# One channel's last group of rows transposed by DMA, the taps folded by ScalarE, and GpSimd's work for a pair in portions of 128 columns

## The reference

```
x      (64, 128, 2048) fp32         batch, channel, time
W      = weights[condition]          one of 16 matrices of 128 x 128 for each batch
x      = x + einsum('bct,bcd->bdt', x, W)
# a diagonal state space layer, for each channel h, with 64 complex modes n:
dtA    = (-exp(log_A_real) + 1j * A_imag) * exp(log_dt)
Ct     = (C[...,0] + 1j*C[...,1]) * (exp(dtA) - 1) / A
K[h,l] = 2 * Re sum_n Ct[h,n] * exp(dtA[h,n] * l)        l = 0..2047
y      = causal convolution of x with K over time, + x * D[h]
y      = y where the time is below the batch's length, else 0
out    = x + y
```

## Time and profile before

| | |
|---|---|
| median of 3 runs | 1088.93 us (1088.23 to 1088.96) |
| the profiled execution | 1082.12 us, its span 1080.3 us |
| granted TensorE clock | 0.996 |
| TensorE busy | 1004.6 us, 93% of the span |
| VectorE busy | 772.3 us, 71% |
| ScalarE busy | 548.5 us, 51% |
| GpSimd busy | 502.7 us, 47% |
| moved by DMA | 304.96 MB, mean 282 GB/s |

### The profile page before, as it was taken

One profiled execution on the slowest core, in us unless ns is written; L12 is line 12 of the kernel. 1 busy time (PEld: TensorE's weight loads), 2 busy tenths in 40 slices (PEclk: granted clock), 3 DMA queues, 4 the chain that ended last, 5 costly groups with the idle time before them and its releaser, 6 DMA issues.

```text
span 1080.3 us, 29253 instructions
## 1 busy us (share of the span) xinstructions
PE 1004.6 (93%) x11632; PEld 739.8 (68%) x11632; DVE 772.3 (71%) x1711; ACT 548.5 (51%) x1166; POOL 502.7 (47%) x545
## 2 busy tenths in 40 slices
PE   8977788777899999999999999999999999999998
PEld 5322234233347888888888788888888888888886
DVE  4989940000017888888888888888888888888885
ACT  2634334244444556556456555555555555555553
POOL 2200042101205556656666665665665665665530
PEclk9999999999999999999999999999999999999999
DMA  8999999999989999999999999999999999999994
GB/s 343 423 423 423 424 422 422 377 424 424 423 326 294 284 271 262 228 227 224 217 239 233 214 238 224 225 234 228 222 232 226 234 221 229 225 225 232 208 223 118
DMA packets 169543, 304.96 MB, mean 282 GB/s; under 512 B 78194, under 2 KB 111346, under 8 KB 161218
## 3 DMA queue, kind: packets, MB, share of 16 engines
q1 hardware_dynamic: 169090, 302.64, 98.4%
q10 hardware_dynamic: 160, 0.26, 0.1%
q0 software_dynamic: 160, 0.20, 0.1%
HBM read 152.37 MB, written 134.41 MB: 265 GB/s over the span
## 4 chain that ended last, share of the span: by engine, by line
PE 74%; DMA 18%; ACT 3%; DVE 2%; issue 2%; SPq 1%; ACTq 0%
DMA u_scratch<-stage 17%; PE bank L590 16%; PE bank L599 15%; PE bank L555 13%; PE bank L541 10%; PE bank L529 7%; PE bank L567 7%; PE bank L596 5%; ACT stage L708 2%; DVE x_t L1001 1%; PE bank L608 1%; DMA x_f<-in_x 1%; DVE st_sb L991 0%; ACT ring L708 0%; DVE u_t L986 0%
## 5 line engine op out<-in xcount | busy, mean ns | idle before, releaser
L590 PE MATMUL bank<-toep,u_t 128*128 128x192 f16 (+1 forms) x3072 | 342.7, 220 | 2.0 <-issue 1.8
L599 PE MATMUL bank<-g_sb,st_sb 128*128 128x256 f16 x1536 | 305.9, 273 | 0.5 <-issue 0.4
L529 PE MATMUL bank<-x_f,w_buf 128*128 128x512 f32 x512 | 237.3, 608 | 57.2 <-ACT stage L708 35.5
L541 PE MATMUL bank<-ident,u_row 128*128 128x128 f32 x1024 | 277.4, 274 | 0.2
L730 ACT ACTIVATE st_sb<-bank 128x128 f16<-128x128 f32 x448 | 123.8, 276 | 289.6 <-PE bank L567 198.0
L590 PEld LDWEIGHTS bank<-toep,u_t 128*128 128x128 f16 x3072 | 231.3, 98 | 16.3 <-issue 2.4
L529 PEld LDWEIGHTS bank<-x_f,w_buf 128*128 128x128 f32 x512 | 93.4, 192 | 192.4 <-issue 109.8
L1016 DVE COPY_PREDICATED o_sb<-mask,u_row 128x512 f32<-128x512 uint8 x256 | 205.8, 804 | 16.6 <-issue 16.5
L986 DVE SCALAR_TENSOR_TENSOR u_t<-bank,u_t 128x512 f16<-128x512 f32 x256 | 176.2, 689 | 37.4 <-ACT u_t L722 35.4
L596 PE MATMUL bank<-toep,x_t 128*128 128x64 f16 x2048 | 188.3, 193 | 1.9 <-issue 1.9
L431 POOL TENSOR_TENSOR lam_sb<-eyes,lam_v 128x512 f16<-128x512 f16 x64 | 75.2, 1176 | 235.7 <-PE bank L567 235.7
(11 more groups left out here) (135 smaller groups left out, 912.6 us busy)
## 6 DMA issues: line engine op xcount, KB each, us to landing
x_f<-in_x SPq DMA_DIRECT2D x64, 1024.0 KB, 19.6
u_row<-u_scratch SPq DMA_DIRECT2D x128, 512.0 KB, 5.7
out<-o_sb SPq DMA_DIRECT2D x254, 256.0 KB, 3.8
u_scratch<-stage SPq DMA_DIRECT2D x50, 1024.0 KB, 17.8
toep<-k_scratch SPq DMA_DIRECT2D x64, 256.0 KB, 6.0
u_scratch<-ring SPq DMA_DIRECT2D x13, 512.0 KB, 14.7
u_scratch<-kept SPq DMA_DIRECT2D x10, 448.0 KB, 7.0
gt_sb<-g_sb SPq DMA_TRANSPOSE x124, 5.4
```

Source lines behind the costliest of these rows:

```text
L529: last = pe.matmul(bank[:, 4 * (n % 2) + k, :], w_buf[n % XS][:, :], x_f[n % XS][:, k * 512:(k + 1) * 512], start=True, stop=True)
L541: last = pe.transpose(bank[:, 4 + q, g * P:(g + 1) * P], u_row[c % 4][:, h, g, tb * P:(tb + 1) * P], ident[:, :])
L590: pe.matmul(bank[:, y, col + tb * P + NM:col + Q], u[:, h, tb, a, rows_], t[:, h, b, NM:Q - tb * P], start=first, stop=False, skip_group_c ...
L599: last = pe.matmul(bank[:, y, col:col + Q], st[:, h, a, gr * ROWS:(gr + 1) * ROWS], g[:, h, b, :], start=False, stop=(m == 2), skip_group_ ...
```

## The change

Four things are done.

1. For the pairs from `TURNED` = 3 on, channel h = 0 (`TH` = 1) no longer has its last group (g = 3) transposed by TensorE: `groups(c, h)` gives 3 instead of 4, and k = 3 and k = 7 return at once. Instead ScalarE (`parts_hi`) and VectorE (`parts_lo`) make the two fp16 parts of these 128 rows x 256 columns from `u_row` into a buffer `parts` of 128 x 512, and SP issues a DMA transpose of it into `u_t` (`transpose_parts`), in slot c for pair c + 1. `inputs_to_state` and the first `first_half` wait for it (`s_pt`). The evacuations of q = 0 and q = 1 take 384 columns instead of 512.
2. `fold_toeplitz` goes from VectorE to ScalarE.
3. GpSimd's operations of a pair are issued in portions of 128 columns: 8 products and 4 subtractions in `outer`, 4 in `outer_lo`, 4 in `make_lambda`, instead of 4, 1, 1 and 1.
4. The orders of ScalarE and VectorE change: ScalarE has "p" and "t" ahead of the pair's first state; VectorE has the two "x" and "p" ahead of it, and "u" (c + 1, 0) and "o" (c - 1, 0) behind the first and second state.

```diff
+TURNED = 3
+TH = 1
+        parts = sb("parts", [P, TH, 2, 2, P], F16)
+        def groups(c, h):
+            return NG - 1 if c >= TURNED and h < TH else NG
...
+            def transpose_parts(c):
+                sp.wait_ge(s_pl, c - TURNED + 1)
+                wait(sp, s_out, 4 * (c - 3))
+                sp.dma_start(ap(u_t[c % 4], (NG - 1) * ROWS, [[NG * ROWS, TH * 4], [1, ROWS]]),
+                             parts[:, :, :, :, :].rearrange("p h b a t -> p (h b a t)"), transpose=True)\
+                    .then_inc(s_pt, 16)
...
+                if TURNED <= c + 1 < PAIRS:
+                    transpose_parts(c + 1)
                 if has(i, c - 1):
                     store_out(i, c - 1, 0)
...
+            PORTIONS = [(h, z) for h in range(2) for z in range(2)]
             def outer(i, c):
-                    for h in range(2):
+                    for h, z in PORTIONS:
                         o = (2 * n + h) * 16
-                        pool.tensor_tensor(out=ap(dst[r], h * Q, [[16, 16], [1, 16]]),
-                                           in0=ap(ta, o, [[1, 16], [0, 16]]),
-                                           in1=ap(tb, o, [[0, 16], [1, 16]]), op=MUL).then_inc(s_gx, 1)
+                        pool.tensor_tensor(out=ap(dst[r], h * Q + z * P, [[16, 8], [1, 16]]),
+                                           in0=ap(ta, o + 8 * z, [[1, 8], [0, 16]]),
+                                           in1=ap(tb, o, [[0, 8], [1, 16]]), op=MUL).then_inc(s_gx, 1)
...
             def transpose_u(i, c, k):
+                if g >= groups(c, q // 2):
+                    return
...
             def inputs_to_state(i, c):
                 pe.wait_ge(s_ul, 4 * n + 4)
+                wait(pe, s_pt, 16 * (n - TURNED + 1))
...
+            def parts_hi(c):
+                for h in range(TH):
+                    act.wait_ge(s_row[c % 4][h], 16 * (c // 4 + 1))
+                wait(act, s_pt, 16 * (c - TURNED))
+                act.activation(parts[:, :, :, 0, :],
+                               u_row[c % 4][:, 0:TH, NG - 1, :].rearrange("p h (b t) -> p h b t", t=P),
+                               ACT.Copy, scale=US).then_inc(s_ph, 1)
...
-                         ("o", c - 1, 0), ("s", c, 1), ("s", c, 2), ("u", c + 1, 1), ("s", c, 3),
+                         ("o", c - 1, 0), ("p", c + 1, 0), ("t", c, 0), ("s", c, 1), ("s", c, 2), ("u", c + 1, 1), ("s", c, 3),
...
+            def parts_lo(c):
+                dve.wait_ge(s_ph, c - TURNED + 1)
+                dve.scalar_tensor_tensor(out=parts[:, :, :, 1, :],
+                                         in0=u_row[c % 4][:, 0:TH, NG - 1, :].rearrange("p h (b t) -> p h b t", t=P),
+                                         scalar=US, in1=parts[:, :, :, 0, :], op0=MUL, op1=SUB).then_inc(s_pl, 1)
...
             def first_half(i, c, part):
                     dve.wait_ge(s_ul, 4 * n + 4)
+                    wait(dve, s_pt, 16 * (n - TURNED + 1))
...
-                steps = (("s", c - 1, 7), ("u", c, 3), ("o", c - 2, 3), ("t", c, 0), ("u", c + 1, 0),
-                         ("o", c - 1, 0), ("s", c, 1), ("x", c, 0), ("s", c, 2), ("x", c, 1), ("s", c, 3),
+                steps = (("s", c - 1, 7), ("u", c, 3), ("o", c - 2, 3), ("x", c, 0), ("x", c, 1), ("p", c + 1, 0),
+                         ("s", c, 1), ("u", c + 1, 0), ("s", c, 2), ("o", c - 1, 0), ("s", c, 3),
```

## The result

The changed kernel takes 1100.1 us (median of 16 runs, 1090.2 to 1108.8) where the kernel before takes 1088.1 (16 runs beside them, 1083.1 to 1092.7): a ratio of 1.0099, interval 1.0075 to 1.0124. One of the changed kernel's runs, the 1108.8, was a slow one and is not in the ratio. Ratios here are formed from the single runs, so they can differ by 0.1 to 0.2% from the quotient of two medians. The forecast was 1083.2, faster. The profiled execution has 1093.7 us of span where before had 1080.3, 13.4 us more.

The account below looks back on a forecast made before the run. TensorE's order of matmuls was taken as the bound; -13.3 (transposes) + 5.1 (late landings) + 2.5 (one early slot) = -5.7 us, so 1088.9 became 1083.2 us, range 1071 to 1103.

Parts of the forecast that it names:

- The transposes: TensorE, pairs 3 to 63: two line 541 transposes fewer in each of 61 pairs, 0.109 us each, -13.3 us.
- ScalarE's pieces: ScalarE's high part and tap fold, ahead of the pair's first state: 0.4 us each, covered by its 1.40 us wait.
- the shorter evacuation: ScalarE: two of four evacuations lose 128 of 512 columns, some 0.1 us each.
- VectorE's low part: VectorE gains the low part, at most 0.69 us, and loses the 1.03 us fold, ending with less work.
- GpSimd at 10 us a pair: GpSimd's 20 portioned instructions take 10 us a pair, between 6.2 and 11.8, fit under 11.4 and cost nothing.
- the fold: VectorE's tap fold, 1.03 us just after a GpSimd subtraction ends, read as waiting for that whole instruction.
- Does the DMA have room for it?: Doubtful step on the DMA engines: about 1.0 us free in a pair; the new transfer takes 0.6, so fits.
- The pair of 12.05 us: Early pair, line 555 at 324.36 and 336.41, taken to carry 0.58 MB more for only 0.4 us.
- The late landings: New DMA transpose landing late: one pair in six by 0.5 us, +5.1 us, and one early slot, +2.5 us.
- the one named for the DMA engines: Rival: DMA engines become the bound through a second hold, 0.55 us a pair, about 1112 us; chance 0.14.
- its sign of recognition: Profile sign of the DMA rival: waits for that DMA in most pairs, landings of 7 us and more on all queues.
- A hold of the engines at each place of a DMA transpose: DMA engines: a second transpose place in each pair, if it makes its own hold, costs 0.3 to 2.4 us.

Follow-up runs that it names:

- e1: The changed kernel with GpSimd's seven whole instructions to a pair again instead of portions: 1146.1 us, ratio 1.059 to the kernel before.
- e3: The kernel before with an added DMA transpose of 128 x 512 fp16 that nobody reads, behind the load of the taps: 1093.7 us, ratio 1.0099.
- e4: The kernel before with the same 128 KB moved by an unread plain DMA copy in the same place: 1088.7 us, ratio 1.0066.
- e7: The changed kernel with output stores cut to the first of four groups, three quarters of the output unwritten: 1064.5 us.
- e8: The kernel before with output stores cut to the first of four groups, three quarters of the output unwritten: 1075.3 us.
- e12: The changed kernel with its DMA transpose from pair 9 on, still behind the taps, and channel 1's store ahead of the table's transposes: 1087.2 us, ratio 1.0065 to before.
- e13: The changed kernel with all transposes on TensorE and channel 1's store ahead of the table's DMA transposes from slot 8 on: 1073.1 us, ratio 0.992 to before.
- e5: The changed kernel with the DMA transpose of the parts from pair 9 on instead of pair 3: 1088.0 us, ratio 1.0034 to the kernel before.
- e10: The kernel before with an unread DMA transpose of 128 x 512 fp16 directly ahead of the table's two: 1095.5 us, ratio 1.0056.
- e14: The changed kernel with channel 1's store, then the parts' DMA transpose, directly ahead of the table's, from pair 9 on: 1063.3 us, ratio 0.984 to before.

## Why the prediction was wrong

**Right.** The transposes: -13.3 forecast, 61 x 0.20 = -12.2 seen. ScalarE's pieces at 0.4 us each: 0.415 both; the shorter evacuation 0.11 less. VectorE's low part under 0.69: 0.53. GpSimd at 10 us a pair: 333.6 us for 682 instructions, 20 to a pair, make 9.8. It is not the bound; the wait for a lambda buffer shrank to 1.5 us a pair and stayed. That VectorE waits for whole GpSimd instructions was read rightly from the fold, and e1 shows what it can cost: with whole instructions the new order is at 1.059. The trace bears out the rule of the Trainium skill (SBUF — State Buffer, SBUF: two separate sides) that I had cited for it: a predicated copy that starts just behind such an instruction takes 1.75 us, where the median is 0.74.

**The step that failed** is the one under "Does the DMA have room for it?": "about 1.0 us is free in a pair", and the new transfer "0.6, inside the 1.0". It was worked out from means. 270 GB/s in early slots at 12.05 us a pair showed that the bytes fit; it did not show when they land, nor what the extra time of those pairs was. (The pair of 12.05 us lies ahead of the stretch of 270 GB/s; the four pairs of line 555 from 336.41 to 384.68 take 12.07 each, so the figure stands.) One of these four has an issue wait of 1.52 us, at 361.13, and between 600 and 1000 us before has three groups of issue waits, 1.4 us in 4 times, beside the 1.8 us of the earlier trace rows. The forecast took issue waits at nothing, before and after, without a reason. e3 prices the step by itself: with nobody waiting, +1.0%, 11 to 13 us. e4 shows that even the plain copy costs 0.7%, and e7 with e8 that with less to store the change gains.

**What I did not think of** is that TensorE also gets its instructions over these DMA engines. The profile's queue list shows it; here two microseconds just before the issue wait at 669.24 (packets, MB, share):

```profile
q1 hardware_dynamic: 751, 0.37, 110.0%
...
q8 instruction: 1, 0.02, 3.0%
```

The one packet of the instruction queue ends at 667.83, and TensorE stands from 668.22 to 669.24. Queue 8 brings 94 packets of 16,384 bytes in both kernels. The traces have 24,232 records of TensorE before and 24,049 after (matmuls, loads and its sequencer's waits for semaphores), so one packet to 258 or 256 of them; no other engine has a tenth as many. And TensorE stops at just these steps. Two stretches from one stop to a later one, in the table of stages:

```profile
505.50:566.30 60.80, 58.21 (x856) 49.40 (x857) 49.03 (x115) 37.46 (x95) 52.02 (x107) 1.00 1.07 239
...
669.20:705.60 36.40, 33.77 (x490) 28.19 (x490) 28.08 (x66) 21.13 (x54) 28.98 (x60) 1.00 1.07 235
```

These are 1713 and 980 matmuls and loads, 7 and 4 times some 245; with the semaphore waits, which this table does not count, they are 1792 and 1024 records, 7 and 4 times 256. The changed kernel's 15 issue waits, and the one of 1.5 us that the profile puts down to ScalarE's `o_sb` (834.22), all lie whole multiples of 256 records apart. The same holds in all sixteen traces of this case: their 101 issue waits of matmuls over 0.25 us between 337 and 1075 us stand at one place in the count of 256, and each ends 1.2 to 1.6 us after a packet of queue 8 has ended. So the issue waits are waits for TensorE's next instructions. The 34 to 36 us between some of them are four such packets. The Trainium skill (Advanced Engine Details and Errata, ISA Cache) gives TensorE a cache of 128 KB and 256 instructions to a line of 16 KB, and the trace agrees with its packets of 16,384 bytes and its steps of 256 records. That the waits grow and shrink with the load and the order of the DMAs is shown by e3, e7, e12 and e13. What holds up the single packet is not shown.

**The late landings** were in the forecast: one pair in six late by 0.5 us, 5.1, and 2.5 for one early slot. For the steady pairs the size came out, 5.3 us, though as five waits of 0.3 to 1.7 us and not ten of 0.5, which is in part luck. The early slots were mis-sized, and in another place: the forecast had its one late landing at the pair behind the taps of 403.56, where none was seen, and the two waits, 0.92 and 4.24 us, came at the first pair with the change and two pairs later (361.95 and 390.63). These two bring the low clock as well, 3.9 us, so that the early slots cost 9.1 instead of 2.5 us; the forecast took a wait of TensorE at its own length. e5, without those slots, is 0.6% better than the change. The two kinds of wait are not apart from each other either: in e12, 13 of the 16 waits for the parts over 0.25 us end 1.3 to 1.8 us after a packet of queue 8 has ended, while 22 of all its 56 pairs from 420 us on (these among them) start within 2 us behind one. What ties them together is not shown.

**The sum again.** -12.2 for the transposes, +20.3 for all waits over those of before (27.9 - 7.6), +3.9 for the low clock behind the two landings: +12.0 of the 13.4 us of span. The clock fell once more, behind the longest issue wait, 2.75 us at 1035.13; from there to the second transpose behind it 1.55 us passed, where the same matmuls at 505.52 took 0.98, and over the 2.8 us of low clock that makes an estimated 1 us. The little that remains lies outside 337 to 1075 us or in waits too short for these views. Of the rivals, the one named for the DMA engines was the right one in kind, though its sign of recognition was only half right: landings did not get much longer (the taps' median is 6.3 us, 6.0 before), and no wait of most pairs appeared. A hold of the engines at each place of a DMA transpose was not what I could show to cost: e3 against e4 does not resolve it, and e10 does only in part. The rule of the Trainium skill (Advanced Engine Details and Errata, X-Bar Transpose (TRN2)) that such transposes are as fast as regular DMAs, which I weighed against the trace, is therefore neither confirmed nor refuted by the difference of e3 and e4 (0.3%, with overlapping intervals).

**Still open:** why the moved store takes the issue waits away and lengthens the landing of the parts, and what the portions alone gain.

## What to carry to other kernels

A share of the DMA engines near 1 is to be taken as a bound until a transfer that nobody reads has been added and timed: means over stages say that bytes fit, not that landings and instruction fetches come in time. Before giving work to a full queue, look for its place in the order, and for that of its neighbours: the unread transfer cost 1.0% behind the loads and still 0.6% ahead of the table's, and only with a store moved ahead as well was nearly nothing left of its price (e14 against e13). It should also stay out of the stretch in which the queue carries something extra. Where the engine that sets the pace shows waits without a releaser, count its instructions between them: here it was always a multiple of 256, however far apart the waits lay in time.

## What the runs showed of the hardware

- TensorE can pay twice for a wait: after waits of 1.19 and 0.92 us close behind each other, and of 4.24 us, twelve matmuls took 4.12 and 4.64 us instead of 2.43, at a granted clock of 0.86 and 0.72 in their stretches. Single waits of up to 1.7 us from 600 to 1000 us left it at 1.00.
- TensorE's instructions come by DMA, in packets of 16,384 bytes on a queue of their own, one to 256 of its records. When DMA is loaded they come late: all 101 waits without a releaser over 0.25 us in sixteen traces (337 to 1075 us) stand at steps of 256 and end 1.2 to 1.6 us after such a packet. In the changed kernel they are 15.9 us in 15 times, in e14, with the same transfers from pair 9 on and in another order, 1.8 us in one.
- VectorE can wait for a whole GpSimd instruction: beside one of 512 columns and 1.27 us a predicated copy took 1.75 us, where the median is 0.74. In the same order of VectorE the whole instructions (256 and 512 columns) give 5.9% over before, portions of 128 give 1.0%.
- A DMA transpose of 128 x 512 fp16 takes SP 1.23 us to issue (median) and lands after 6.1 us behind the loads, and after 4.5 us when it is issued ahead of the table's DMA transposes.
